# Projections of layer 1: gathers placed between GpSimd's differences, and the token gates applied by ScalarE

## What is computed

```python
x = x + gb * _L0_ffn_ref(h, ...)        # layer 0: top-1 of 8 experts, times the token's gate
...
h = _layernorm(x, axis=-1) * (1 + ca) + sa
x = x + ga * _L1_attn_ref(h, ...)       # layer 1: q, k, v from low-rank projections, q and k with rotary terms
```

## Time and profile before

| | us |
|---|---|
| median of 3 runs | 1167.91 |
| lowest, highest | 1163.81, 1169.43 |
| the profiled execution | 1166.31 |
| its span, first to last instruction | 1164.2 |

### The profile page before, as it was taken

The page is one execution under the profiler, slowest core; times in us unless marked ns, Lnnn a source line. Parts: engine busy times, 40 slices in busy tenths (PEclk is TensorE's granted clock), DMA queues, the critical chain, the costliest instruction groups (busy, mean ns, idle before and its releaser), DMA issues. The chain is left out here.

```text
span 1164.2 us, 23750 instructions
## 1 busy us (share of the span) xinstructions
PE 1044.9 (90%) x9028; PEld 493.3 (42%) x9028; DVE 948.4 (81%) x1442; ACT 780.3 (67%) x1559; POOL 329.8 (28%) x467
## 2 busy tenths in 40 slices
PE   6987699587678999999999999999999989889997
PEld 4786599443321222222222222222222229657655
DVE  7976555478889999999999999999999808966555
ACT  4543434144423999999999999999999984543421
POOL 4732367667520000000000000000000007347463
PEclk9998899898976999999999999999999999999999
DMA  7011276319980012220222101220120000423322
GB/s 242 1 37 37 87 202 203 107 34 213 202 222 1 8 30 35 35 35 3 35 35 36 28 10 35 35 34 17 22 35 3 2 3 3 158 79 98 93 62 81
DMA packets 94119, 76.81 MB, mean 66 GB/s; under 512 B 42900, under 2 KB 72980, under 8 KB 93496
## 3 DMA queue, kind: packets, MB, share of 16 engines
q1 hardware_dynamic: 89144, 65.33, 24.0%
q0 software_dynamic: 4864, 9.97, 3.4%
HBM read 47.74 MB, written 27.46 MB: 65 GB/s over the span
## 5 line engine op out<-in xcount | busy, mean ns | idle before, releaser
L1464 DVE TENSOR_REDUCE mx<-p_psA 128x1 f32<-128x1024 f32 x512 | 585.3, 1216 | 9.2 <-PE p_psA L1627 9.2
L1555 ACT ACTIVATE p_pt<-p_psS 128x512 f32<-128x512 f32 x1024 | 548.3, 597 | 37.7 <-PE p_psS L1649 18.0
L1662 PE MATMUL p_acc<-p_pt,V 128*32 128x256 f32 x4096 | 328.4, 392 | 15.4 <-ACT attn L1546 13.8
L1627 PE MATMUL p_psA<-K,Q 48*128 48x512 bf16 x1024 | 319.9, 395 | 9.4 <-DVE mx L1464 7.8
L1649 PE MATMUL p_psS<-Q,K 51*128 51x512 bf16 x1024 | 310.0, 384 | 0.0
L1662 PEld LDWEIGHTS p_acc<-p_pt,V 128*32 128x32 f32 x4096 | 82.0, 108 | 210.9 <-ACT p_pt L1555 110.4
L1381 POOL TENSOR_TENSOR mr<-zeros,mx 128x16 f32<-128x16 f32 x32 | 7.1, 221 | 546.9 <-DVE mx L1464 546.9
L1627 PEld LDWEIGHTS p_psA<-K,Q 48*128 48x128 bf16 x1024 | 57.1, 95 | 232.6 <-DVE mx L1464 197.7
L1649 PEld LDWEIGHTS p_psS<-Q,K 51*128 51x128 bf16 x1024 | 62.8, 93 | 18.1 <-ACT p_pt L1555 12.6
L1069 DVE TENSOR_TENSOR f_h<-f_bank,b 128x512 f32<-128x512 f32 x40 | 27.7, 692 | 38.2 <-PE f_bank L1137 38.2
L1029 ACT ACTIVATE f_h1T<-f_h 128x512 f32<-128x512 f32 x40 | 25.2, 629 | 31.5 <-DVE f_h L1069 31.5
(11 more groups left out here) (336 smaller groups left out, 1437.4 us busy)
## 6 DMA issues: line engine op xcount, KB each, us to landing
f_w<-in_w SPq DMA_DIRECT2D x40, 256.0 KB, 3.2
Q<-q_rows SPq DMA_DIRECT2D x32, 192.0 KB, 4.6
K<-k_rows SPq DMA_DIRECT2D x32, 192.0 KB, 5.1
hrows<-h SPq DMA_DIRECT2D x8, 512.0 KB, 3.2
result<-f_shared_kept SPq DMA_DIRECT2D x12, 256.0 KB
result<-f_y SPq DMA_DIRECT2D x10, 256.0 KB, 3.5
V<-v_rows SPq DMA_DIRECT2D x16, 144.0 KB, 5.6
x<-in_x SPq DMA_DIRECT2D x4, 512.0 KB, 5.6
```

The source lines that it names most:

```text
L1464: dve.tensor_reduce(mx[v % 2][:, h, qt:qt + 1], psA[t][:], AX.X, ALU.max).then_inc(a_max, 1)
L1555: act.activation(pt[s % 2][:, head_at(s, j), :], psS[k % 3][:], ACT.Exp, scale=INV_SCALE).then_inc(s_out, 1)
L1627: mm = pe.matmul(psA[t][:, c * 512:(c + 1) * 512], Q[g % NBUF][rows, pair, q0:q0 + P], K[g % NBUF][rows, pair, c * 512:(c + 1) * 512], sta ...
L1662: mm = pe.matmul(acc[VW * h:VW * (h + 1), cols], V[g % NBUF][:, kc, h * (HD + 1):h * (HD + 1) + VW], pt[s % 2][:, h, cols], start=(kc == 0 ...
```

## The change

On POOL the four indirect transfers of `gather(m + 4)` no longer stand behind the three differences: one is issued before the first, one between the first and the second, one between the second and the third, one behind. The wait for the gather before stands ahead of the first of them. On ACT a new function `weigh(c)`, for half batches 2 to 7, waits for the gathered rows and for the combination of half batch c - 2 and multiplies the four tiles by their gates, four activations of 128x128; it stands behind `reduced(m + 1)` and ahead of the first part of q. On DVE, from half batch 2 on, one multiplication of 128x512 by `gb` in place takes the place of the four, and waits for ACT's new semaphore `gated`.

```diff
--- before.py
+++ after.py
@@ -1231,6 +1231,7 @@
                                                            n.sem("ct_ready"), n.sem("u_mm"))
         k_mm, v_mm, v_out, bias_mm = n.sem("k_mm"), n.sem("v_mm"), n.sem("v_out"), n.sem("bias_mm")
         bv_ready = n.sem("bv_ready")
+        gated = n.sem("gated")
         full_ready, part1, rest1, part2, part3 = ([n.sem(f"{x}{q}") for q in "qk"] for x in ("full_ready", "part1_", "rest1_", "part2_", "part3_"))
         qk_stored, v_stored = M.qk_stored, M.v_stored
         ones, nmr, bvs = n.sb("ones", [MROWS, L], BF16), n.sb("nmr", [P, NT]), n.sb("bvs", [P, P])
@@ -1328,11 +1329,13 @@
             def _(pool):
                 link = Link(pool, pool_step)
 
-                def gather(c):
-
-                    if c >= 1:
+                def gather(c, first=0, last=4):
+
+                    if c >= NM:
+                        return
+                    if c >= 1 and first == 0:
                         pool.wait_ge(gathered[c - 1], 64)
-                    for i in range(4 * c, 4 * c + 4):
+                    for i in range(4 * c + first, 4 * c + last):
                         pool.indirect_dma_start(
                             out=M.h[:, i, :], out_offset=None, in_=M.result0[:, :],
                             in_offset=bass.IndirectOffsetOnAxis(ap=M.slot[:, i:i + 1], axis=0)).then_inc(gathered[c], 16)
@@ -1347,14 +1350,17 @@
                 def half(m):
 
                     j = slice((m % 2) * 512, (m % 2) * 512 + 512)
+                    gather(m + 4, 0, 1)
                     pool.wait_ge(rest1[0], m + 1)
                     pool.wait_ge(part2[0], m + 1)
                     pool.tensor_tensor(parts[m // 2 % 2][2][:, 0, j], rest[:, 0, :], parts[m // 2 % 2][1][:, 0, j], ALU.subtract).then_inc(part3[0], 1)
+                    gather(m + 4, 1, 2)
                     pool.wait_ge(full_ready[1], m + 1)
                     pool.wait_ge(part1[1], m + 1)
                     if m >= 1:
                         pool.wait_ge(part3[1], m)
                     pool.tensor_tensor(rest[:, 1, :], full[:, 1, :], parts[m // 2 % 2][0][:, 1, j], ALU.subtract).then_inc(rest1[1], 1)
+                    gather(m + 4, 2, 3)
                     pool.wait_ge(part2[1], m + 1)
                     pool.tensor_tensor(parts[m // 2 % 2][2][:, 1, j], rest[:, 1, :], parts[m // 2 % 2][1][:, 1, j], ALU.subtract).then_inc(part3[1], 1)
 
@@ -1368,8 +1374,7 @@
                     if m + 2 < NM:
                         rstd(m + 2)
                     half(m)
-                    if m + 4 < NM:
-                        gather(m + 4)
+                    gather(m + 4, 3, 4)
 
                 link = Link(pool, at_step)
                 for v in range(NUNITS):
@@ -1392,10 +1397,16 @@
 
                     t0, t1, w = 4 * c, 4 * c + 4, 4
                     b = t0 // TB
-                    dve.wait_ge(gathered[c], 64)
-                    for i in range(t0, t1):
-                        ins = dve.scalar_tensor_tensor(out=weighed[:, i % TB, :], in0=M.h[:, i, :], scalar=M.gate[:, i:i + 1],
-                                                       in1=M.mod[:, 0, b, GB * P:(GB + 1) * P], op0=ALU.mult, op1=ALU.mult)
+                    gb = M.mod[:, 0, b, GB * P:(GB + 1) * P]
+                    if c < 2:
+                        dve.wait_ge(gathered[c], 64)
+                        for i in range(t0, t1):
+                            ins = dve.scalar_tensor_tensor(out=weighed[:, i % TB, :], in0=M.h[:, i, :], scalar=M.gate[:, i:i + 1],
+                                                           in1=gb, op0=ALU.mult, op1=ALU.mult)
+                    else:
+                        dve.wait_ge(gated, c - 1)
+                        rows = weighed[:, t0 % TB:t0 % TB + w, :]
+                        ins = dve.tensor_tensor(rows, rows, gb.unsqueeze(1).to_broadcast([P, w, P]), ALU.mult)
                     link(ins)
                     xb = M.x[:, t0:t1, :]
                     link(dve.tensor_tensor(xb, xb, weighed[:, t0 % TB:t0 % TB + w, :], ALU.add))
@@ -1475,6 +1486,14 @@
                         ins = act.activation(xn[m % 2][:, t, :], M.x[:, i, :], ACT.Identity, bias=nmr[:, i:i + 1], scale=M.rstd[:, i:i + 1])
                     ins.then_inc(xn_ready, 1)
 
+                def weigh(c):
+
+                    act.wait_ge(gathered[c], 64)
+                    act.wait_ge(var_ready, c - 1)
+                    for i in range(4 * c, 4 * c + 4):
+                        ins = act.activation(weighed[:, i % TB, :], M.h[:, i, :], ACT.Copy, scale=M.gate[:, i:i + 1])
+                    ins.then_inc(gated, 1)
+
                 def modulated(m):
 
                     act.wait_ge(xn_T, m + 1)
@@ -1520,6 +1539,8 @@
                     values(m)
                     if m + 1 < NM:
                         reduced(m + 1)
+                    if m + 2 < NM:
+                        weigh(m + 2)
                     split(m, 0)
                     second(m, 0)
                     if m + 2 < NM:
```

## The result

| | before, us | after, us |
|---|---|---|
| median | 1167.91 (5 runs) | 1182.69 (5 runs) |
| lowest, highest | 1163.81, 1169.43 | 1181.66, 1184.93 |
| span of the profiled execution | 1164.2 | 1180.6 |

The ratio of the medians is 1.0137, 95% interval 1.0122 to 1.0152: slower by 14.8 us. The forecast was 1182, range 1171 to 1192.

The account below looks back on a forecast made before the run. DVE was taken to bound the kernel, its head maxima starting when it leaves the projections. Terms 10.5 + 2.8 + 0.95 = +14.2 us on 1166.3 gave 1180.5; with the median 1.6 above, 1182, range 1171 to 1192.

Parts of the forecast that it names:

- The ring: Layer 1 projections: waits from modulation through PE, ACT's weighing, DVE and POOL to next modulation; 13.79 us, 14.50 with gathers.
- Weighing: ACT, behind its reduction: four activations of 128x128, priced like L1475's four at 1.65 us per half batch, inside the ring.
- POOL's line: POOL in half batches 0 to 3: two gathers of 1.24 us ahead of the key difference delay it 0.71 us.
- Landing wait: POOL, ahead of the first gather: waits for all the previous gather's rows; +2.8 us in all, bounds 0 and 8.1.
- Clock: PE's reduction in the ring: one case at lowered clock, 2.08 instead of 1.13 us; +0.95, bounds none and 5.7.
- the last rival: POOL stalls for landings in every half batch, up to half the reductions at low clock (2.9): +21.5 us, 1189; 18%.
- The keys' sum undisturbed: DVE's keys' L1428 starts at 9.79, before POOL's first difference at 10.38, so it takes its undisturbed 0.69 us.
- One to one to the end: Head maxima begin when DVE leaves the projections, so a later stage end delays the program's end by the same amount.
- the weighing fits beside: Rival: ACT finishes weighing before DVE leaves the queries' sum, saving 8.1 us in the middle: about 1160; 7%.
- the delay is swallowed: Rival: the heads' start hangs on something other than DVE, so a later stage end costs nothing: 1168; 7%.
- always short: Rival: gathers land in 2.6 us as in half batch 3, so POOL's stall is 0: +11.4 us, 1179; 20%.

Follow-up runs that it names:

- the halves: Changed kernel with only the gathers spread: ratio 1.0044 to the kernel before; changed kernel with only the weighing moved to ACT: ratio 1.0090.
- the dose: Changed kernel with ACT's weighing done twice in each of six half batches, first into an unread spare tile: ratio 1.0185 to the kernel before.
- later_wait: Changed kernel, but each gather waits for the landing of the gather two before it instead of one before: ratio 1.0114 to the kernel before.
- weigh_first: Changed kernel with ACT's weighing moved to the top of its half batch, ahead of the modulation: ratio 1.0043 to the kernel before.
- spread_only: Changed kernel with only the gathers spread, DVE weighing the rows as before: ratio 1.0044 to the kernel before.
- spread_later_wait: Kernel before with gathers spread, each waiting for the landing of the gather two before; DVE weighs as before: ratio 1.0016 to the kernel before.

## Why the prediction was right

**The ring.** The forecast put 14.50 us on each of four half batches and 13.79 on two, 85.58 in sum, with 2.8 for landings and 0.95 for the clock beside it; it was 92.86 in the profile. DVE waits for ACT's weighing in every half batch, as said, and the halves, the dose and the move show the place of the weighing to be the larger cause. Term by term:
- *Weighing*: 1.26 to 1.27 instead of 1.65; L1475, from which the price came, has a shift besides the scale, these activations have none. Six times 0.39 less: -2.3.
- *POOL's line*: the key difference came at 12.64 instead of 12.77, but that is luck. The weighing had put everything 0.39 earlier, and from the rest of q to the key difference it was 12.64 - 7.26 = 5.38 instead of 12.77 - 7.65 = 5.12. Over the four half batches with gathers this part was 1.8 us longer than forecast, stalls aside: L1347 took 1.41 to 1.43 instead of 1.06, and one gather 1.42 instead of 0.94.
- *Landing wait*: 0.67 and 3.38, less the usual 0.16 of issue, 3.7 us against 2.8, in the half batches named (1 and 3). Right, and later_wait takes it away.
- *Clock*: three slow reductions where I added one: 2.85 instead of 0.95. Mis-sized; the 2.9 of the last rival was the better figure.
- *The keys' sum undisturbed*: right in half batches 0 to 3. In 4 and 5 it took 1.48 and 1.44, because the step took POOL's first difference to be due at 10.38 everywhere; without a gather ahead of it, it is due at 9.14, before the sum (332.52 against 332.79). 1.5 us more.
So 85.58 - 2.3 + 1.8 + 3.7 + 2.85 + 1.5 = 93.1, 0.3 above the 92.86; half batches 4 and 5 were each 0.1 shorter than this.

**One to one to the end.** The heads did start later by the full amount, 18.5 us, 0.7 of them from ahead of the stage. Yet the span grew by 16.4: from the first maximum to the end it took 827.7 instead of 829.8 us. The last exponential keeps its distance to the first maximum within 0.3 us (956.5 and 975.3), so this lies in the unchanged stages behind, where single profiles differ. The other 1.6 us between 16.4 and the measured 14.8 is that the profiled execution of the kernel before was 1.6 below its median, that of the changed kernel the median itself. The forecast of +14.2 for a measured +14.8 is therefore better than its terms, and so close by luck: they came to 14.2 for a stage whose six distances grew by 17.8 in the profile on the first chip, and by 14.5 on the later ones.

**The rivals.** That the weighing fits beside is refuted by DVE's 27.1 us of waits for it; that the delay is swallowed, by the maxima, which began 18.5 us later and brought the end with them. Landings were neither always short nor always long: 0 to 3.4 us of stall, and up to 5.1 in weigh_first.
The Trainium skill's constant for a transfer from POOL ("DMA: Bandwidth & Descriptors", section "Anatomy of one DMA — SWDGE (gpsimd) path") would have left no stall. POOL's waits show otherwise: the gather issued from 284.66 on, in a stage where the transfer engines were busy at a share of 0.73, took 7.1 to 10.6 us to land, and the measurement decides.

## What to carry to other kernels

Before moving work to an engine that is idle half of the time, find the instruction behind which it will stand and ask when the engine gets there: 1.3 us of work in each of six half batches cost 11 us behind a late reduction, and the same work some instructions earlier in the program a fraction of that. A transfer spread between other instructions takes its waits along; put the wait where nothing urgent queues behind it, and look at what the new order makes the other engines run beside.

## What was not expected of the hardware

DVE's sum of two tiles in SBUF met POOL's differences in a worse way than in the earlier trace rows, where 1.64 us was the longest. It took 2.21 to 2.23 us in 21 cases over eight profiles (and 2.16 in one more, in spread_only at 280.76). In each of the 21 it began 0.46 to 0.49 us behind the start of a gather, and a difference followed the gather at once and began while the sum was running: in spread_later_wait as shown, and twice in the changed kernel (at 256.81 and 287.52), where DVE's idle time hid it.
The Trainium skill, page "SBUF — State Buffer", section "Who interferes with whom", says that a DVE instruction with two SBUF inputs contends with a GpSimd instruction that reads SBUF, and that the order of issue decides who blocks. The trace agrees that one waits for the other, but here the sum that started first by the profile waited for the difference. The gather alone doesn't hold it: the sum at 253.97 above began with the gather of 253.95, was over before the difference at 255.00, and took 0.70. Why the difference wins when it follows a gather is not shown.
